# Three 16-head attentions: score blocks in quarters of 64x64, stack loads in halves, bank pairs in turn

## The reference, cut to what matters

```python
# layer 1: biased by the distance ("alibi")
att = einsum('bhqd,bhkd->bhqk', q, k) / sqrt(8) + where(causal, slopes * rel, -inf)
y = einsum('bhqk,bhkd->bhqd', softmax(att), v) @ w_proj.T
# layer 2: q and k turned by position ("rope8"), 4 key heads for 16 query heads
scores = where(causal, einsum('bqhd,bkhd->bhqk', rope(q), rope(k)) * 8**-0.5, -inf)
out = einsum('bhqk,bkhd->bqhd', softmax(scores), v) @ Wout + bout
# layer 3: 8 content features and 32 turned ones, 40 in all ("latent")
scores = q_content @ k_content.T + rope(q_rope) @ rope(k_rope).T, causal, scaled, softmax, times v
```

## Time and profile before

| | |
|---|---|
| median of 3 runs | 2914.24 us (2912.7 to 2918.39) |
| profiled execution | 2911.34 us, span 2909.5 us |
| busy in the span | PE 79%, PEld 51%, DVE 53%, ACT 39%, POOL 22% |
| mean granted TensorE clock | 0.885 |
| alibi, rope8, latent attention | about 1342 to 1657, 1943 to 2259, 2423 to 2888 us |

### The profile page before, as it was taken

How to read it: one execution, slowest core, us unless ns; L and a number is a source line. 1 busy time by engine, 2 the same in 40 slices (tenths; PEclk the granted TensorE clock), 3 DMA queues, 4 the chain that set the end, 5 groups by cost and what they waited for, 6 DMA issues and landing times. The chain is left out here.

```text
span 2909.5 us, 54198 instructions
## 1 busy us (share of the span) xinstructions
PE 2305.2 (79%) x18107; PEld 1476.4 (51%) x18108; DVE 1535.6 (53%) x5386; ACT 1138.6 (39%) x1810; POOL 637.8 (22%) x689
## 2 busy tenths in 40 slices
PE   4487999997699999784888828447888866999997
PEld 1133777773267777431444416324554313777775
DVE  4635666635466665435677313147775245565663
ACT  5623554433244544333555402133554340233333
POOL 0204434300244342002010040421110012221210
PEclk8796999998899999896999869767999865899999
DMA  2000000000000000001222140202221002333330
GB/s 109 0 0 1 1 1 0 0 1 0 0 1 2 0 0 1 1 4 45 70 80 67 55 150 0 62 28 81 73 74 33 0 33 90 92 111 91 91 110 30
DMA packets 81241, 115.82 MB, mean 40 GB/s; under 512 B 10352, under 2 KB 67184, under 8 KB 77720
## 3 DMA queue, kind: packets, MB, share of 16 engines
q1 hardware_dynamic: 79024, 109.48, 12.4%
q0 software_dynamic: 2048, 4.20, 0.5%
HBM read 69.70 MB, written 42.86 MB: 39 GB/s over the span
## 5 line engine op out<-in xcount | busy, mean ns | idle before, releaser
L1240 ACT ACTIVATE at_pr<-ps 128x768 f32<-128x768 f32 x384 | 312.1, 813 | 505.7 <-PE ps L1176 505.7
L1282 DVE CUSTOM_DVE_ANT_0 at_junk<-ps,conf 128x128 f32<-128x128 f32 x768 | 220.1, 287 | 235.7 <-PE ps L1158 216.0
L1284 DVE CUSTOM_DVE_ANT_0 at_junk<-ps,conf 128x256 f32<-128x256 f32 x768 | 321.4, 419 | 0.0
L1158 PE MATMUL ps<-at_ks,at_qs 40*128 40x128 f32 (+5 forms) x2048 | 223.0, 321 | 70.7 <-DVE at_m L1284 26.9
L1170 PE MATMUL ps<-at_qs,at_ks 41*128 41x256 f32 (+5 forms) x2048 | 199.5, 294 | 58.2 <-DMA at_qs<-at_ml 28.4
L693 POOL TENSOR_TENSOR la_tc<-la_ta,la_tb 128x512 f32<-128x512 f32 x128 | 162.3, 1268 | 354.6 <-DVE la_tb L959 354.6
L710 PE MATMUL ps<-w_l0f,la_hs 128*128 128x512 f32 x256 | 152.5, 680 | 54.4 <-POOL la_hs L675 36.3
L1170 PEld LDWEIGHTS ps<-at_qs,at_ks 41*128 41x128 f32 (+2 forms) x2048 | 140.9, 145 | 105.9 <-ACT at_pr L1240 53.5
L860 ACT ACTIVATE la_pr<-ps 128x640 f32<-128x640 f32 x128 | 90.2, 705 | 265.8 <-PE ps L762 265.4
L1191 PE MATMUL ps<-at_pr,at_v 128*32 128x256 f32 (+1 forms) x3072 | 175.8, 341 | 16.4 <-issue 15.7
L1158 PEld LDWEIGHTS ps<-at_ks,at_qs 40*128 40x128 f32 (+2 forms) x2048 | 104.9, 151 | 160.3 <-DVE at_m L1284 59.2
(11 more groups left out here) (308 smaller groups left out, 4995.6 us busy)
## 6 DMA issues: line engine op xcount, KB each, us to landing
scratch_latent<-at_parts SPq DMA_DIRECT2D x32, 640.0 KB, 4.8
at_qs<-scratch_latent SPq DMA_DIRECT2D x32, 320.0 KB
at_ks<-scratch_latent SPq DMA_DIRECT2D x32, 320.0 KB
scratch_alibi<-at_parts SPq DMA_DIRECT2D x32, 192.0 KB, 2.3
at_ks<-scratch_alibi SPq DMA_DIRECT2D x192, 32.0 KB
scratch_rope<-at_parts SPq DMA_DIRECT2D x32, 192.0 KB, 2.3
at_ks<-scratch_rope SPq DMA_DIRECT2D x192, 32.0 KB
moe_weights<-in_moe SPq DMA_DIRECT2D x1, 4096.0 KB, 20.7
```

The costliest lines, as they stand in the source:

```text
L1158: m = nc.tensor.matmul(o[:, cols:cols + keys], q[:, block_q:block_q + P], kk[:, 0:keys], start=True, stop=True)
L1240: nc.scalar.activation(pr[:, p % RING, :, :], ps[:, 6:8, 0:384], ACT.Exp, scale=scale).then_inc(s.at_prob, 1)
L1282: nc.vector.tensor_tensor_reduce(junk[:, x % 2, e, 0:P], ps[:, m + e, 0:P], k.cf("late")[:, P:2 * P], 1.0, BIG, ALU.add, ALU.max, m2[:, r, ...
L1284: last_max = nc.vector.tensor_tensor_reduce(junk[:, x % 2, e, P:3 * P], ps[:, m + e, P:3 * P], k.cf("late"), 1.0, BIG, ALU.add, ALU.max, m ...
```

## The change

It does these things in all three attentions:

- `scores` and `keyed` use quarters: 64 columns of weights instead of 128, 64 partitions of the output each (c = 0, 1), so eight matmuls a set instead of four. The masks are four matmuls on 64 rows with 256 moving columns, from new constants "causal_q_x" and "causal_k_x" beside the old ones.
- In the bf16 layers scores and keyed share three bank pairs (2-3, 4-5, 6-7) in turn, the score mask is added on TensorE too, and VectorE takes two plain reductions a pass. The latent layer keeps one pair each and the mask with the maximum on VectorE.
- The stack loads are cut in halves of 4 heads (`stack_loads(n, g)`), each half with its own semaphore. SyncE's step is now: half 0 of row i-1, the rows of maxima, half 1, the stores. 18 DMAs a half in the bf16 layers, 4 in the latent one.
- Small work moves: `shifts` to x=0, `value_rows` to x=2, `turn` to x=6, alibi's product to x=4, the latent products to (0, 1) at x=2, (2, 3) at x=4 and 4 at x=6. The copy to oT goes from ScalarE to VectorE, the one to S from VectorE to ScalarE.

```diff
+    crossed = [(name + "_x", np.roll(a, P // 2, 0)) for name, a in (("causal_q", causal), ("causal_k", causal.T))]
...
+        def score_bank(n, x):
+            return 2 + 2 * ((n + 2 * x) % 3) if deep else 2
+
+        def keyed_bank(n, x):
+            return 2 + 2 * ((n + 2 * x + 1) % 3) if deep else 6
...
+            def load_half(i, n, g):
+                r, nr = i - 1, (n - 1) % slots
+                sem = (s.at_stacked0, s.at_stacked1)[g]
+                if g == 0:
+                    sp.wait_ge(s.at_scratch, 32 * (row0 + r + 1))
+                    sp.nop(nofuse=True)
+                at_least(sp, sem, 16 * (sd0 + nst * r))
+                sp.nop(nofuse=True)
+                if live(i, 1 + slots):
+                    at_least(sp, s.at_keyed, HP * (row0 + r - slots) + HP // 2 * (g + 1))
+                    sp.nop(nofuse=True)
+                for dst, src in a.stack_loads(nr, g):
+                    sp.dma_start(dst, src).then_inc(sem, 16)
+
             def step(i, n):
+                if live(i, 1):
+                    load_half(i, n, 0)
                 if live(i, 3):
                     sp.wait_ge(s.at_mt, row0 + i - 2)
...
                 if live(i, 1):
-                    r, nr = i - 1, (n - 1) % slots
-                    sp.wait_ge(s.at_scratch, 32 * (row0 + r + 1))
...
-                    for dst, src in a.stack_loads(nr):
-                        sp.dma_start(dst, src).then_inc(s.at_stacked, 16)
+                    load_half(i, n, 1)
                 if live(i, 0):
                     a.wait_parts(sp, i)
...
+            def quarter_masks(bank, name):
+                for c in range(2):
+                    for e in range(2):
+                        r = slice(64 * e, 64 * e + 64)
+                        rows = k.cb(name if c == e else name + "_x")[r, :]
+                        out = ps[64 * c:64 * c + 64, bank + e, 0:3 * P].rearrange("p (b t) -> p b t", t=P)[:, 0:3:2, :]
+                        m = nc.tensor.matmul(out, k.cb("ident", 64 * e, 64)[r, :], rows.unsqueeze(1).to_broadcast([64, 2, P]),
+                                             start=False, stop=True, skip_group_check=True)
+                return m
+
             def scores(i, n, x):
-                u = HP * (row0 + i) + x
                 if x == 0:
-                    pe.wait_ge(s.at_stacked, 16 * (sd0 + nst * (i + 1)))
-                at_least(pe, s.at_max, u - deep + 1)
+                    pe.wait_ge(s.at_stacked0, 16 * (sd0 + nst * (i - 1)))
+                if x == HP // 2:
+                    pe.wait_ge(s.at_stacked1, 16 * (sd0 + nst * (i - 1)))
+                if deep:
+                    at_least(pe, s.at_prob, keyed_until(i, x, 2))
+                    if isinstance(i, int):
+                        at_least(pe, s.at_max, scored_until(i, x, 3))
+                else:
+                    at_least(pe, s.at_max, scored_until(i, x, 1))
+                pe.nop(nofuse=True)
+                bank = score_bank(n, x)
                 for block_q, cols, keys in ((0, 0, P), (P, P, 2 * P)):
-                    for e in range(2):
-                        q, kk = stacks(n, x, e, stack_rows)
-                        o = ps[:, 2 + 2 * (x % deep) + e, :]
-                        m = nc.tensor.matmul(o[:, cols:cols + keys], q[:, block_q:block_q + P], kk[:, 0:keys],
-                                             start=True, stop=True)
+                    for c in range(2):
+                        for e in range(2):
+                            q, kk = stacks((n - 2) % slots, x, e, stack_rows)
+                            m = nc.tensor.matmul(ps[64 * c:64 * c + 64, bank + e, cols:cols + keys],
+                                                 q[:, block_q + 64 * c:block_q + 64 * c + 64], kk[:, 0:keys],
+                                                 start=(cols == 0), stop=not split, skip_group_check=True)
+                if split:
+                    m = quarter_masks(bank, "causal_q")
                 m.then_inc(s.at_score, 1)
...
+                        if split:
+                            nc.vector.tensor_reduce(m2[:, r, 0, x:16:8], ps[:, at:at + 2, 0:128], AX.X, ALU.max, negate=True)
+                            m = nc.vector.tensor_reduce(m2[:, r, 1, x:16:8], ps[:, at:at + 2, 128:384], AX.X, ALU.max,
+                                                        negate=True)
...
-    def stack_loads(n):
-        loads = []
+    def stack_loads(n, g):
+        loads, w = [], HP // 2 * L
         for e in range(2):
-            cols = slice(e * HP * L, (e + 1) * HP * L)
+            cols = slice((2 * e + g) * w, (2 * e + g + 1) * w)
             q, kk = (scr[n, j].rearrange("s (d h) t -> (s d) (h t)", h=H16)[:, cols] for j in range(2))
-            at = lambda stack, lo, hi: stack[64 * e + lo:64 * e + hi, n, :]
+            at = lambda stack, lo, hi: stack[64 * e + lo:64 * e + hi, n, g * w:(g + 1) * w]
             loads += [(at(a.Qs, 0, 24), q[0:24]), (at(a.Qs, 24, 40), q[0:16]), (at(a.Qs, 40, 48), q[0:8])]
             loads += [(at(a.Ks, 8 * j, 8 * j + 8), kk[8 * m:8 * m + 8]) for j, m in enumerate((0, 0, 0, 1, 1, 2))]
...
-    PRODUCTS = {2: 0, 3: 1, 4: 2, 5: 3, 6: 4}
+    PRODUCTS = {2: (0, 1), 4: (2, 3), 6: (4,)}
```

More of the change, by code:

```diff
@@ L1160, in scores @@
+                if split:
+                    m = quarter_masks(bank, "causal_q")
                 m.then_inc(s.at_score, 1)
             def keyed(i, n, x):
-                u = HP * (row0 + i) + x
-                if x == 0:
-                    pe.wait_ge(s.at_mrow, 16 * (md0 + nm * (i + 1)))
-                at_least(pe, s.at_prob, u)
-                for keys, cols, first in ((0, 0, 0), (P, 2 * P, P)):
-                    for e in range(2):
-                        q, kk = stacks(n, x, e, last)
-                        nc.tensor.matmul(ps[:, 6 + e, cols:cols + L - first], kk[:, keys:keys + P], q[:, first:L],
-                                         start=(cols == 0), stop=False, skip_group_check=True)
@@ L1173, in keyed_masks @@
-            def keyed_masks():
-                for e in range(2):
-                    for cols in (0, 2 * P):
-                        m = nc.tensor.matmul(ps[:, 6 + e, cols:cols + P], k.cb("ident"), k.cb("causal_k"), start=False,
-                                             stop=(cols > 0), skip_group_check=True)
-                m.then_inc(s.at_keyed, 1)
+                row, p = 3 + (x < KEY_LAG), (x - KEY_LAG) % HP
+                if p == 0:
+                    pe.wait_ge(s.at_mrow, 16 * (md0 + nm * (i - row + 1)))
@@ new lines, in keyed @@
+                if deep:
+                    at_least(pe, s.at_max, scored_until(i, x, 1))
+                    if isinstance(i, int):
+                        at_least(pe, s.at_prob, keyed_until(i, x, 3))
+                else:
+                    at_least(pe, s.at_prob, keyed_until(i, x, 1))
+                pe.nop(nofuse=True)
+                bank = keyed_bank(n, x)
+                for keys, cols, first in ((0, 0, 0), (P, 2 * P, P)):
+                    for c in range(2):
+                        for e in range(2):
+                            q, kk = stacks((n - row) % slots, p, e, last)
+                            nc.tensor.matmul(ps[64 * c:64 * c + 64, bank + e, cols:cols + L - first],
+                                             kk[:, keys + 64 * c:keys + 64 * c + 64], q[:, first:L],
+                                             start=(cols == 0), stop=False, skip_group_check=True)
@@ L1180, in values @@
+                quarter_masks(bank, "causal_k").then_inc(s.at_keyed, 1)
             def values(i, n, x):
@@ L1198, in step @@
                     if live(i, 2):
-                        scores(i - 2, (n - 2) % slots, x)
-                    row = 3 + (x < KEY_LAG)
-                    if live(i, row):
-                        keyed(i - row, (n - row) % slots, (x - KEY_LAG) % HP)
-                        keyed_masks()
+                        scores(i, n, x)
+                    if live(i, 3 + (x < KEY_LAG)):
+                        keyed(i, n, x)
                     if live(i, 5) and x == 0:
                         turn_back(i)
-                    if live(i, 3) and x == 1:
+                    if live(i, 3) and x == 0:
                         shifts(i, n)
@@ L1229, in step @@
                 for x in range(HP):
[L1230 removed]
+                    if live(i, 4) and x == 5:
                         act.wait_ge(s.at_attended, HP * (b - 3))
@@ L1302, in step @@
-                    if live(i, 4) and x == 7:
+                    if live(i, 4) and x == 6:
                         dve.wait_ge(s.at_turn, b - 3)
```

175 lines of the change are left out of this document (95 added, 80 removed).

## The result

The changed kernel takes **3123.31 us** (median, 3105.16 to 3129.19) beside 2913.47 of the kernel before: ratio 1.0707 [1.0661, 1.0753]. The forecast of 3042 us had the sign and the place right and the size too small; 3123 lies past its range. The profiled execution takes 3123.13 us, span 3121.3.

What follows compares the result with a forecast made beforehand. It took SyncE's in-order DMA queue to bound the bf16 stages: alibi +52, rope8 +58, tail -10, latent +27, constants +0.5, sum +127.5, so 3042 us. Range: 2975 less 10, to 3095 plus some of latent's +50.

Steps and rivals of the forecast that it cites:

- Issues: SyncE queue, bf16 stages: a half-size load issue costs the same 0.345 us, so 18 more issues are 6.2 us a row.
- rival (a): SyncE in `load_half`: issue price falls with size, rows about 13 us, kernel faster at about 2835; chance 0.08.
- Exposed landing of the stores: SyncE before half 0, bf16 stages: the wait for the stores, hidden before, stands bare at 2.88 us a step.
- A wait that the order adds: bf16 stores wait for parts made behind the mask-row wait at x=4: 0.6 us a step alibi, 1.4 rope8; bounds 0 and 3.
- The step in all: One bf16 row: SyncE queue loop of 18.7 us plus the wait for parts, 0.6 in alibi and 1.4 in rope8.
- Rival (b): bf16 stages: the queue's wait rests TensorE, its clock falls, steps of 21 and 22 us, about 3095; chance 0.17.
- Rows of 13 us without the queue: bf16 stages, if issues got cheaper: rows paced by VectorE and TensorE at about 13 us.
- SyncE has 5 us to spare: Rope8 stage before the change: a heads pass is held by TensorE, exp and maxima, leaving SyncE 5 us to spare.
- TensorE in the bf16 stages covered: Quarter matmuls at 1.2 us a pass make TensorE 17 us a row, under the queue's 18.7, so no cost.
- Latent: Latent stage: quarters and masks together 0, but paired products expose waits for the maximum: +1.9 us a row, +27; bounds 0 and +50.

Runs made afterwards that it cites:

- e1: Changed kernel, but bf16 stack loads whole again (18 DMAs a row) and behind the mask rows; 2922.3 us.
- e3: Kernel before, with each bf16 stack load cut into two of half size in one block behind the mask rows, 36 a row; 3139.4 us.
- e16: e15 with the mask-row DMAs of the bf16 attentions issued by ScalarE (passes 1 and 2); 2885.7 us.
- e17: Kernel before, with its mask rows issued by ScalarE at passes 1 and 2 instead of SyncE; 2897.3 us.
- e4: Changed kernel, but the latent attention's five products stand one a pass again (x=2 to 6); 3097.2 us.
- e6: Changed kernel with the edits of e1 and e4 together: whole loads behind the mask rows, latent products one a pass; 2907.0 us.
- e15: e6 with the row loop of the bf16 attentions making one turn instead of three, other rows written out; 2889.6 us.
- e18: Changed kernel with mask rows issued by ScalarE, latent products one a pass, and one turn of the bf16 row loop; 2929.6 us.
- e5: Changed kernel, queue as it is, but the bf16 parts made at pass 3 (rope8 products at 2 and 3), ahead of the waiting pass; 3058.9 us.
- e7: Kernel before, with six K loads merged into three DMAs that repeat their source, 12 issues a row instead of 18; 2998.4 us.

## Why the prediction fell short

- *Issues*: right at best. Six loads of 16 KB take 1.99 us, the same as six of 32 KB; from 320 down to 16 KB the price does not fall, so rival (a) fell. But some groups drag (half 0 takes 6.2 to 7.4 us), and with the gap before the mask rows the two halves are 0.9 us a row over the sum in alibi and 0.7 in rope8.
- *Exposed landing of the stores*: 2.88 forecast, 3.11 in the row shown, but 3.8 and 3.5 in the means, up to 5.6 (1599.97 to 1605.22 is 5.25). Another 0.9 and 0.6 us a row.
- ***"A wait that the order adds"***: **the step that failed**. 0.6 us a step in alibi and 1.4 in rope8 were taken, with a bound of 3. SyncE waited 17.7/9 = 2.0 us a row for the parts in alibi (3.0 in the row shown, gap included) and 44.3/11 = 4.0 in rope8. I let the parts' chain run through pass 4 at warm passes of 1.6 to 2.1 us and took 8.1 us for it in rope8; it took 10.8. It runs behind a rest of TensorE of 5.5 us, at 0.80 of the clock over the alibi stage instead of 0.99. No run parts the lower clock from the rest that comes before it.
- *The step in all*: 22.4 and 23.8 us instead of 19.3 and 20.1. Of the 3.1 us in alibi the late parts are 1.5, of the 3.7 in rope8 they are 2.7; landing and dragging issues are the rest, less 0.2 to 0.3 that the mask rows took under their price. Times 13 it is +40 and +48, against +36 and +47 missed in the stages.
- *Rival (b)* had this very mechanism, at 21 and 22 us and 3095, with a chance of 0.17. Its argument against ("in the steady rows now it keeps 0.99 with 81% busy") was read from the kernel whose order lets TensorE run through. I had worked out that TensorE would idle 2 to 5 us in one place, and should have priced the passes behind that rest at the slow level.
- *Rows of 13 us without the queue* and *"SyncE has 5 us to spare"*: wrong (e1, e3, e16, e17). With the mask rows off the queue rows are still 15.5 to 16.8 us in the mean (e17, e16), and the mask-row loop of before lies just above that.
- *TensorE in the bf16 stages covered*: right in effect, wrong in price. The bound was 1.2 us a pass. Warm, scores, keyed and all masks, 24 quarter matmuls, run from 1599.57 to 1600.32, 0.75 us; in the trace of before the 12 of a pass take 0.83 (1508.28 to 1509.11). By the rule of the Trainium skill, TensorE: Matmul & The Clock Gate, section Weight-path perf modes, the fast weight load needs 128 weights. This trace does not speak against it: a load of 64 bf16 columns is recorded at 102 to 108 ns in that set, one of 128 at 92 to 99 in the set of before, so half the columns save no time. But the set as a whole is not longer for it.
- *Latent*: mechanism right, and the row too (+1.8 us, forecast +1.9), but in part by luck. The waits grew by 2.8 us a row (four of 0.76 for one of 0.20) where 2.0 was taken, and the quarters, priced at 0, give about 1.0 back. The stage came to +16.7 and not +27, since the second row is 4 us shorter and rows i = 9 and 12, long in both kernels, hardly grow; one other row is 7 us longer, cause not known. e4 shows 14 of it undone by spreading. The Trainium skill, TensorEngine Tiling (Array Packing), section Overview, promises up to twice the rate; for these f32 sets of 40 rows this trace shows 0.67 us from 0.76.
- *Not forecast*: the jump back of the longer loop, 17 us in e6 against e15. In the change itself TensorE stands there too (9.3 us in two places from 1500 to 1700 us), but the queue covers it: no row stands out, and e18's bf16 stages gain nothing by one turn.

## What to carry to other kernels

When a transfer is issued earlier on an in-order queue, look first at what is moved behind it: here 18 loads ahead of four tiny mask-row copies cost 141 us, the 18 extra issues themselves 60. Follow the wait round: if the engine that is made to rest also produces what the queue waits for next, the wait comes back to the queue (at least 64 of the 141 us, e5), and what comes right behind the rest is to be priced at the clock that its trace shows there (here 1.52 us for value products of 0.87). And before giving an idle queue credit for its gaps, ask whether a gap is spare or is the part of its loop that runs elsewhere.

## What the runs showed that was not expected

- The three K loads of e7, two with a repeated source, take 1.93 us to issue, as long as the six that they merge, and the scores x=0 start 4.2 us after the last issue instead of 1.8.
- Sets of 64x64 quarters in bf16 are not longer than the ones of 128 columns that they replace. With whole loads, spread latent products and one turn, the rest of the change (quarters, bank pairs, masks on TensorE, moved small work) and the one turn gain 23 us together; they were not parted.
- Behind a jump back of the row loop an engine stands 4 to 5 us: TensorE at two rows of the alibi stage of e6 and at one of its rope8 stage (22.1 us), VectorE in the latent stage of the kernel before, where the row grows by 7.6 us.
- ScalarE can issue the four mask-row DMAs of a row (2.6 us) and the kernel gains by it (e17), though in e17 its next exp waits 1.6 us a row behind them.
